# Attention steps: the next half's projections placed ahead of the product of values with probabilities

## The reference, cut to what matters

```python
q = rope(norm(x) @ Wq.T);  k = rope(ctx @ Wk.T);  v = ctx @ Wv.T    # 32, 8, 8 heads
attn = softmax(mask(q @ k.T * scale))                               # 128 x 128 for each head and batch
x = x + tanh(g) * (concat(attn @ v) @ Wd.T)
x = x + tanh(g) * ffn(norm(x))
```

## Time and profile before

| | |
|---|---|
| runs | 2069.57, 2072.62, 2073.32 us; median 2072.62 |
| profiled execution, and its span | 2071.37 us, 2069.6 us |
| TensorE busy, matmuls | 1886.9 us (91%), 9480 |
| VectorE, ScalarE, GpSimd busy | 1383.0 (67%), 837.5 (40%), 1011.6 us (49%) |
| granted clock of TensorE, mean | 0.964 of 2.4 GHz |
| DMA, share of 16 engines | 10.9% |
| chain that ended last | PE 27%, POOL 24%, issue 23%, DVE 18%, ACT 7% |

### The profile page before, as it was taken

How to read it: one execution, slowest core, us unless ns; L and a number is a source line. 1 busy time by engine, 2 the same in 40 slices (tenths; PEclk the granted TensorE clock), 3 DMA queues, 4 the chain that set the end, 5 groups by cost and what they waited for, 6 DMA issues and landing times.

```text
span 2069.6 us, 28274 instructions
## 1 busy us (share of the span) xinstructions
PE 1886.9 (91%) x9480; PEld 1517.7 (73%) x9480; DVE 1383.0 (67%) x2563; ACT 837.5 (40%) x2428; POOL 1011.6 (49%) x808
## 2 busy tenths in 40 slices
PE   5999999878878999999999998779999999999987
PEld 4777777656457878878878776668787787878866
DVE  6555555566775776776776777757767767677675
ACT  3455554531323444443444443134444434434441
POOL 2122231334246565565665655166656657557551
PEclk9999999988679999999999999889999999999999
DMA  4000010020101010110110101011101101001001
GB/s 172 20 20 27 13 40 1 16 88 0 38 11 46 26 46 20 35 35 16 50 35 15 56 21 34 1 33 50 35 15 51 35 15 51 25 25 51 26 6 41
DMA packets 37142, 69.48 MB, mean 34 GB/s; under 512 B 4394, under 2 KB 6186, under 8 KB 36946
## 3 DMA queue, kind: packets, MB, share of 16 engines
q1 hardware_dynamic: 37074, 68.61, 10.9%
HBM read 66.50 MB, written 2.10 MB: 33 GB/s over the span
## 4 chain that ended last, share of the span: by engine, by line
PE 27%; POOL 24%; issue 23%; DVE 18%; ACT 7%; POOLq 0%; DMA 0%; SPq 0%; DVEq 0%; ACTq 0%
PE ps L346 9%; PE ps L348 8%; PE ps L347 8%; POOL rope_a L1377 7%; POOL q_loL L1389 5%; POOL wq_loL L1354 4%; POOL wo_loL L1354 3%; POOL probs L1394 3%; DVE pt_loL L856 2%; ACT ot_hi L1172 2%; DVE rope_b L830 1%; DVE rope_b L829 1%; DVE stats L751 1%; DVE rope_a L828 1%; DVE negmax L846 1%
## 5 line engine op out<-in xcount | busy, mean ns | idle before, releaser
L1377 POOL TENSOR_TENSOR rope_a<-rope_a,rope_b 128x512 f32<-128x512 f32 x160 | 208.0, 1300 | 383.0 <-DVE rope_b L830 383.0
L1394 POOL TENSOR_TENSOR probs<-probs,rsums 128x512 f32<-128x512 f32 (+1 forms) x160 | 193.9, 1212 | 352.2 <-DVE rsums L852 352.2
L1159 ACT ACTIVATE probs<-ps,nbias 128x128 f32<-128x128 f32 (+1 forms) x640 | 239.8, 387 | 195.8 <-DVE nbias L848 195.5
L346 PE MATMUL ps<-wo_hiL,ot_hi 128*128 128x512 f32 x608 | 254.5, 419 | 20.0 <-POOL wo_loL L1354 8.8
L346 PE MATMUL ps<-xt_hi,wq_hiL 128*128 128x512 f32 x608 | 243.2, 400 | 0.6 <-DVE rope_b L830 0.6
L862 DVE TENSOR_TENSOR ot_lo<-ps,ot_hi 128x512 fp32r<-128x512 f32 (+1 forms) x160 | 106.3, 664 | 202.9 <-ACT ot_hi L1172 145.2
L348 PE MATMUL ps<-wo_hiL,ot_lo 128*128 128x512 f32 x608 | 240.6, 396 | 0.0
L347 PE MATMUL ps<-wo_loL,ot_hi 128*128 128x512 f32 x608 | 240.5, 396 | 0.0
L348 PE MATMUL ps<-xt_hi,wq_loL 128*128 128x512 f32 x608 | 238.9, 393 | 0.0
L347 PE MATMUL ps<-xt_lo,wq_hiL 128*128 128x512 f32 x608 | 238.8, 393 | 0.0
L1152 ACT CAST q_hiL<-rope_a 128x512 fp32r<-128x512 f32 x128 | 79.7, 623 | 299.5 <-POOL rope_a L1377 299.3
(11 more groups left out here) (208 smaller groups left out, 4586.5 us busy)
## 6 DMA issues: line engine op xcount, KB each, us to landing
raw<-in_L_proj SPq DMA_DIRECT2D x108, 256.0 KB, 2.6
raw<-in_L_out SPq DMA_DIRECT2D x76, 256.0 KB, 2.6
raw<-in_F_w SPq DMA_DIRECT2D x16, 256.0 KB, 2.7
x<-in_x SPq DMA_DIRECT2D x8, 256.0 KB, 4.5
ct_raw<-in_ctx_t SPq DMA_DIRECT2D x4, 512.0 KB, 7.6
cn_raw<-in_ctx SPq DMA_DIRECT2D x8, 256.0 KB, 9.1
out<-x SPq DMA_DIRECT2D x8, 256.0 KB, 2.0
raw<-in_L_kv SPq DMA_DIRECT2D x8, 192.0 KB, 2.6
```

The source lines that it names most:

```text
L346: pe.matmul(dst, l_hi, r_hi, start=start, stop=False)
L1159: e = act.activation(probs[:, at_:at_ + L.keys], ps[:, bank + at_ // 512, at_ % 512:at_ % 512 + L.keys], ACT.Exp, bias=nbias[:, b % 2, h:h ...
L1377: gp.tensor_tensor(rope_a[:, a], rope_a[:, a], rope_b[:], ALU.add).then_inc(L.s_rsum, 1)
L1394: gp.tensor_tensor(pv, pv, rsums[:, b % 2].unsqueeze(2).to_broadcast([P, GH, L.keys]), ALU.mult).then_inc(L.s_p, 1)
```

## The change

In each step the projections now stand ahead of PV in TensorE's list. ScalarE and VectorE read the results in the same new order: the evacuations of the step's projections except its last one stand ahead of ot_hi and ot_lo. Nothing is added or removed; GpSimd's and SyncE's lists stay as they are.

```diff
--- before.py
+++ after.py
@@ -554,12 +554,12 @@
                             transposes(b - 1, i)
                         if b >= 2:
                             out_proj(b - 2, i)
+                        if b < 3 or (not last and b < B - 1):
+                            fillers(b, i)
                         if b >= 1:
                             heads_out(b - 1, i)
                         if last and b >= 5:
                             norm_transpose(after, b - 5)
-                        if b < 3 or (not last and b < B - 1):
-                            fillers(b, i)
 
                     if not last:
                         fillers(B - 1, i, only=0)
@@ -887,11 +887,11 @@
                         if b >= 2:
                             residual(b - 2, i)
                         row_sum(b, i)
-                        if b >= 1:
-                            ot_tail(b - 1, i)
                         if b < 3 or (not last and b < B - 1):
                             for k in range(len(L.fill[b]) - 1):
                                 evacuate(b, k, i)
+                        if b >= 1:
+                            ot_tail(b - 1, i)
                         if last and b >= 3:
                             v.wait_ge(L.s_x, B * i + b - 1)
                             norm_step(after, b - 3)
@@ -1189,12 +1189,12 @@
                         exps(b, i)
                         if late and not early:
                             head((b - 1) % 8, len(L.fill[(b - 1) % 8]) - 1, i, NOW if b else BEFORE)
-                        if b >= 1:
-                            o_head(b - 1, i)
                         if b < 3 or (not last and b < B - 1):
                             for k in range(len(L.fill[b]) - 1):
                                 if not (L.rope and b % HALF == 0):
                                     head(b, k, i)
+                        if b >= 1:
+                            o_head(b - 1, i)
                         if b == 0:
                             act.wait_ge(L.s_x, B * i + 1)
                             for h in range(L.chunks):
```

## The result

| | before | after |
|---|---|---|
| median of 6 runs, us | 2071.1 | 2080.17 |
| ratio, 95% interval | | 1.0047 (1.0034 to 1.006) |
| profiled execution, span, us | 2071.37, 2069.6 | 2080.01, 2078.2 |
| mean granted clock of TensorE | 0.964 | 0.959 |

The account below looks back on a forecast made before the run. TensorE was taken as the bound, idling mostly for pt_lo. L2 and L3 loop groups -3.2, their closing groups +0.8 and L0 +2.0 gave -0.4 us on 2071.37; with 1.25 for the median, 2072 us, range 2058 to 2085.

Parts of the forecast that it names:

- Groups of L2 and L3: The 14 loop groups: pt_lo waits go, one ot_lo wait of 1.6 us comes; -0.23 us each, -3.2 us in all.
- step 3: In L2 and L3 loop groups, PV no longer waits for pt_lo: 0.77 us removed.
- step 4: In L2 and L3 loop groups, Wo's product waits 1.6 us for ot_lo; the old 0.82 us wait goes.
- The rival of the late row maximum: Step 4 of L2 and L3: VectorE runs late, so that step gives nothing back; 2083 us, chance 0.17.
- Step 1: In L2 and L3, its removed wait of about 0.5 us gains nothing, becoming a longer wait ahead of Wo's product.
- The clock, as weighed: TensorE's clock in L2 and L3: the new 1.6 us wait is too short to lower it.
- The rival: TensorE's clock falls after the new L2 and L3 wait: +17 to +25 us, about 2092 us, chance 0.04.
- L0: Three loop groups: six ot_lo waits of 0.78 us added, 4.0 us removed; net +0.7 each, +2.0 us with its closing group.
- Closing groups: Step 3 of L2's and L3's last groups: Q3's rope products stand behind ot_lo(1); +0.4 us each, +0.8 in all.

Follow-up runs that it names:

- experiment 5: The full change, but ScalarE keeps ot_hi ahead of the copy of K0 in step 3 of L2 and L3; 2051.84 us against 2069.18 before.
- experiment 8: PV behind the step's first projection in TensorE's list alone, but step 1 of L2 and L3 as in the kernel before; 2043.38 us against 2071.51 before.
- experiment 3: The full change, but step 1 of L2 and L3 keeps the old order on all three engines; 2074.04 us against 2070.1 before.
- experiment 4: The full change, with two heads' scores computed a second time in step 2 of L2 and L3; 2068.27 us against 2070.1 before.
- experiment 1: The new order in L0 alone, L2 and L3 as in the kernel before; 2072.13 us against 2070.1 before.
- experiment 6: The kernel before, with PV behind the step's first projection in TensorE's list alone, in all three layers; 2039.41 us against 2069.18 before.
- experiment 7: The full change, with two heads' scores computed a second time in step 6 of L2 and L3; 2095.59 us against 2071.51 before.

## Why the prediction was wrong

Point by point:
- **Groups of L2 and L3.** Forecast 79.8 us, measured 79.77 to 79.80 in the nine that are neither the first of their layer nor show a fall. The wait for pt_lo went, the wait for ot_lo came once, by the chain through GpSimd and the copy of K0; experiment 5 shows that this place in ScalarE's list alone costs 1.3 us per group. The mechanism is right. That the sum is right to 0.05 us is partly luck: step 3 gained 0.55 us where I had 0.77, and step 4 lost 0.55 (its wait was 1.37, not 1.60) where I had 0.78. The rival of the late row maximum did not strike: the second projection of step 4 starts 2.73 us behind the first, its bare length.
- **Step 1.** "Step 1 is worth nothing": right for the time of what follows, since the product with Wo still starts on GpSimd's release, and experiment 8 has the same groups. But "It only turns into a longer wait" was priced at nil. **This is the step that failed.** The longer idle time let the clock fall: 3 loop groups at 1.4 us and both closing groups at about 1.5 us, 7 us of the 9 that lie between the forecast and the measured time. Experiments 3 and 4 take the pause away in two different ways, and the falls of step 2 go. The traces of all ten kernels say the same. Leave out the first group of each layer, which has no wait for the probabilities in step 2, and each kernel has 14. In the five where that wait is 0.48 to 0.74 us, the clock falls in step 2 of 20 of 70; in the five where it is 0.37 or less (before, experiments 1, 3, 4 and 8), of none of 70. The 7 us are the price of the falls where they stood; in the closing groups experiments 3 and 4 did not win them back.
- **The clock, as weighed.** I compared one new wait, 1.6 us in step 4, with two long single waits of L0. At step 4 the clock did hold. The fall came in step 2, at two waits of 0.73 and 0.57 us with the short matmuls of scores ahead of the first and only the four transposes between them, and it came without any single wait near 1.8 us. The Trainium skill, "TensorE: Matmul & The Clock Gate", section "A second HAM failure mode: psum-queue depth-cycling", tells of such a case in another kernel (frequent short idles between groups of matmuls make the clock oscillate); the trace of after agrees, with 0.50 in the product with Wo. I had set the rule aside because the groups of before ran at 1.00; their pause in step 2 was 0.4 us shorter. The rival was named with 0.04, but with its place at step 4 and in every group.
- **L0.** Forecast +0.7 per group, measured +0.96, from parts that were further off. The new wait ahead of the product with Wo is 0.78 us in each of steps 2 to 7, as reckoned. But I took the 6.6 us that the weight loads stood idle for TensorE's own loss; from start to start the eight waits for pt_lo are 4.5 us. Those of steps 2 to 6 were worth 2.3 us, not 4.0. Step 1 did get shorter (6.44 instead of 7.19 us), and the 0.78 of step 2 only takes that back, since the product with Wo starts there 17.6 us into the group in both kernels; I had counted the 0.78 as a loss and step 1 as nothing. In step 7 the first wait for pt_lo shrank, so it lost 0.44 (19.91 instead of 19.47).
- **Closing groups.** Step 3 of both takes 7.52 instead of 7.14 us: the +0.4 of the forecast. What I left out is that its longer wait, 1.33 us, can bring the clock down too, as experiments 3 and 4 show.
- **The stretch behind L3's closing group** is 2.4 us longer, with no changed instruction in it. The granted clock is 0.68 in 2028 to 2044 after, 0.89 in the matching 2022 to 2038 before. In the eight experiments the stretch from the first scores of L3's closing group to the end ran from 122.3 to 128.3 us, from kernel to kernel. Which share of it is the change's and which the clock's chance isn't settled.

What stays open is what decides when the clock falls. The pause of step 2 is as long in experiments 5 and 6 as in the full change, and none of their groups falls; experiment 7 shows that a shift in time moves and multiplies the falls. So in step 2 of these groups no fall came without the pause, and the pause doesn't suffice.

## What to carry to other kernels

A product that waits for one operand and feeds another engine's chain has two distances, to its input and to its next user; put independent work on both sides of it (here one projection each: 30 us), not all of it ahead. When a copy is moved ahead of another on an in-order engine, look at what the moved copy itself waits for. And a wait that only grows behind an unchanged release need not be free on TensorE: look at the idle time around it, and at the clock, before you price it at nothing.

## What the runs showed of the hardware

In step 2 of L2 and L3 the granted clock of TensorE fell to 0.50, 1.2 GHz, in 20 of 70 groups with a wait of 0.48 to 0.74 us ahead of the four transposes and one of 0.57 to 0.68 behind them; with 0.37 us or less ahead of them it fell in none of 70. In step 4 of a closing group it fell in 5 of the 16 that stood idle for 1.33 and 0.50 us just before, with the three matmuls of PV between. A product with Wo that met a fall took 4.45 instead of 2.90 us. The falls of step 2 hit the same three loop groups in two kernels that share the order of L2 and L3, nine after a shift of 0.67 us per group, and none in kernels whose groups last 78.5 us. The kernel with matmuls added in the pause was 12 us faster than without them.
